# A causal attention kernel whose diagonal score blocks are laid out in quarters of 32 tokens instead of halves of 64

## The reference

```
q, k, v = heads of x @ Wq.T, x @ Wk.T, (x @ Wv.T) * sigmoid(x @ Wg.T)
q, k = rotary(rms_norm(q)) * q_gain, rotary(rms_norm(k));  k, v repeated from 4 to 16 heads
a1 = softmax(mask(q1 @ k1.T / 2)) @ v1      # mask: key <= query
a2 = softmax(mask(q2 @ k2.T / 2)) @ v2
y  = concat(a1 - lambda * a2, a1 + lambda * a2) @ Wo.T
x  = layernorm(x + y)
x  = layernorm(x + ffn(x))                  # three cycles of a small coupling network
```

## Time and profile before

| | us |
|---|---|
| median of 3 runs | 283.04 (281.01 to 283.7) |
| profiled execution, span from first to last instruction | 280.2 |
| its own time | not given |
| TensorE matmuls busy | 251.0 (90%) |
| ScalarE busy | 234.9 (84%) |
| VectorE busy | 200.2 (71%) |
| GpSimd busy | 81.4 (29%) |

### The profile page before, as it was taken

The page is one execution under the profiler, slowest core; times in us unless marked ns, Lnnn a source line. Parts: engine busy times, 40 slices in busy tenths (PEclk is TensorE's granted clock), DMA queues, the critical chain, the costliest instruction groups (busy, mean ns, idle before and its releaser), DMA issues.

```text
span 280.2 us, 8439 instructions
## 1 busy us (share of the span) xinstructions
PE 251.0 (90%) x2959; PEld 110.9 (40%) x2960; DVE 200.2 (71%) x760; ACT 234.9 (84%) x339; POOL 81.4 (29%) x241
## 2 busy tenths in 40 slices
PE   8249899999999999999999999989898999999990
PEld 3033334434344343443434444434343332223890
DVE  1687588696886967869678696773254477999993
ACT  3147899999999999999999999999975777788685
POOL 8540422415234152241522415320111000000473
PEclk9757999999999999999999999999999999999997
DMA  5201751753516526155351650615300175653045
GB/s 130 56 1 20 95 113 36 102 100 92 112 29 140 102 48 150 32 99 106 81 112 37 132 109 23 131 41 91 67 13 0 37 153 121 135 121 74 1 137 165
DMA packets 58072, 23.43 MB, mean 84 GB/s; under 512 B 42785, under 2 KB 56001, under 8 KB 58049
## 3 DMA queue, kind: packets, MB, share of 16 engines
q1 hardware_dynamic: 57760, 23.11, 39.1%
q10 hardware_dynamic: 288, 0.02, 0.1%
HBM read 4.90 MB, written 2.10 MB: 25 GB/s over the span
## 4 chain that ended last, share of the span: by engine, by line
PE 69%; issue 12%; ACT 9%; DVE 4%; DMA 2%; POOL 1%; ACTq 0%; DVEq 0%; POOLq 0%
PE O L589 11%; PE O L595 10%; PE S L713 8%; PE S L502 5%; PE S L512 4%; ACT o_sb L888 3%; PE M L628 3%; PE M L614 3%; PE S L531 3%; PE S L754 2%; DMA qk<-parts 2%; PE S L492 2%; PE S L522 2%; PE M L639 2%; PE S L723 2%
## 5 line engine op out<-in xcount | busy, mean ns | idle before, releaser
L882 ACT ACTIVATE probs_past<-S 128x1024 f32<-128x1024 f32 x64 | 64.5, 1038 | 7.1 <-PE S L492 7.1
L882 ACT ACTIVATE probs_late<-S 128x1024 f32<-128x1024 f32 x64 | 66.4, 1050 | 1.3 <-PE S L502 1.3
L589 PE MATMUL O<-probs_past,values 128*32 128x512 f32 x256 | 34.8, 612 | 7.0 <-ACT o_sb L888 5.8
L882 ACT ACTIVATE probs_early<-S 128x1024 f32<-128x1024 f32 x32 | 32.8, 1027 | 3.7 <-PE S L531 3.7
L595 PE MATMUL O<-probs_late,values 128*32 128x256 f32 x512 | 34.3, 385 | 0.2
L1130 DVE TENSOR_TENSOR roped<-rotated,rstd 128x128 f32<-128x128 f32 (+1 forms) x64 | 12.2, 247 | 26.7 <-POOL rstd L1506 26.5
L1491 POOL TENSOR_TENSOR minus_half_sum<-sum_eps,minus_half 128x40 f32<-128x40 f32 x16 | 4.5, 283 | 80.5 <-DVE estimate L1118 74.8
L1367 DVE SCALAR_TENSOR_TENSOR cY<-coup,ratio,Y 128x256 f32<-128x256 f32 x48 | 21.1, 481 | 5.8 <-ACT coup L966 5.0
L713 PE MATMUL S<-X,cn_w 128*128 128x512 f32 x48 | 25.0, 627 | 0.0
L502 PEld LDWEIGHTS S<-qk 32*64 32x64 bf16 x512 | 8.0, 101 | 34.0 <-issue 34.0
L502 PE MATMUL S<-qk 32*64 32x256 bf16 x512 | 20.2, 292 | 0.2 <-ACT probs_late L882 0.2
(11 more groups left out here) (185 smaller groups left out, 528.1 us busy)
## 6 DMA issues: line engine op xcount, KB each, us to landing
Y<-X SPq DMA_DIRECT2D x48, 128.0 KB, 2.4
xT_in<-in_xT SPq DMA_DIRECT2D x16, 128.0 KB, 2.6
x_res<-in_x SPq DMA_DIRECT2D x16, 128.0 KB, 2.1
out<-result SPq DMA_DIRECT2D x16, 128.0 KB, 1.9
qk<-parts SPq DMA_TRANSPOSE x15, 4.9
future_in<-in_future SPq DMA_DIRECT2D x1, 128.0 KB, 2.7
w_o<-in_w_o SPq DMA_DIRECT2D x2, 64.0 KB, 2.6
cn_w<-in_cn_w SPq DMA_DIRECT2D x2, 64.0 KB, 2.8
```

The costliest lines, as they stand in the source:

```text
L589: mm = pe.matmul(O[32 * g:32 * g + 32, :], values[p][:, 0, g, s, at:at + 32], probs_past[:, s, g, :], start=m == 0, stop=False)
L882: act.activation(dst, S[TILE_BUFFER[n]][:, :, :], ACT.Exp).then_inc(exp_done[n], 1)
```

## The change

The diagonal blocks are cut in quarters of 32 tokens (e = 0 to 3). The second token tile is now stored with its quarters reversed, (3, 2, 1, 0), and the first in order. Nine tiles a batch: the four LATE tiles hold, for both token tiles, the queries of the last quarter (which see all 128 keys) and one more quarter: quarter 2, which sees 96 keys. The 32 partitions of keys left over there take the first quarter of the other token tile, whose queries see only 32 keys. One MIDDLE tile holds quarter 1 (64 keys) of both token tiles for all heads. All constants for masks come in one load of 512 columns for 256; a small constant `own` (1 or 0 by partition, for three mixes) is loaded too. GpSimd's `mix_values` makes three sets of mixed values where `early_copy` made one; `early_values` and `own_half` with their memsets on VectorE go. The loop calls `middle_half` on both sides of `turn_outputs`, before weigh 2, in place of the early pair after it. ScalarE has one exponential less, and copies the heads before the last one. The code below leaves out declarations, constants and the general path.

```diff
+STORED_QUARTERS = ((0, 1, 2, 3), (3, 2, 1, 0))
-TILE_BUFFER = (0, 1, 2, 0, 1, 2, 0, 1, 0, 2)
-TILE_BEFORE = (8, 7, 9, 0, 1, 2, 3, 4, 6, 5)
+TILE_BUFFER = (0, 1, 2, 0, 1, 2, 0, 1, 2)
+TILE_BEFORE = (6, 7, 8, 0, 1, 2, 3, 4, 5)
+            sp.dma_start(own[:, :, :], A["own"]).then_inc(n_["own_loaded"], 16)
...
-            def late_part(p, n, far):
+            def late_quarter(p, n, e):
                 _, s, h = TILES[n]
                 for t in range(T):
+                    at = t * 256 + e * 128
                     for j in range(2):
                         rows = group_rows(2 * h + j)
+                        pe.matmul(S[TILE_BUFFER[n]][:, j, at:at + 128], kT[p][rows, t, s, :],
+                                  quarters(p, rows, t, s)[:, 1 - e if t else 2 + e],
+                                  start=e == 0 and t == 0, stop=False, skip_group_check=True)
+            def first_quarter(p, n):
+                _, s, h = TILES[n]
+                for t in range(T):
+                    of = 1 - t
+                    keys = slice(96, 128) if of == 1 else slice(0, 32)
+                    for j in range(2):
+                        rows = group_rows(2 * h + j)
+                        pe.matmul(S[TILE_BUFFER[n]][keys, j, t * 256:t * 256 + 128], kT[p][rows, of, s, keys],
+                                  qT[p][rows, of, :, s, keys], start=True, stop=False, skip_group_check=True)
...
+            def middle_part(p, n, h):
                 for s in range(2):
                     for t in range(T):
                         for j in range(2):
                             rows = group_rows(2 * h + j)
+                            at = (2 * h + s) * 128
+                            pe.matmul(S[TILE_BUFFER[n]][halves(t), j, at:at + 128], kT[p][rows, t, s, halves(t)],
+                                      quarters(p, rows, t, s)[:, 1 + t], start=s == 0, stop=False, skip_group_check=True)
+            def middle_mask(n, h):
+                for j in range(2):
+                    rows = halves(j)
...
+                    mm = pe.matmul(S[TILE_BUFFER[n]][:, j, h * 256:(h + 1) * 256], middle16[rows, :], quarter,
+                                   start=False, stop=True, skip_group_check=True)
...
+                    late_quarter(p, m, 0)
+                for m in (n, n + 1):
+                    first_quarter(p, m)
+                for m in (n, n + 1):
+                    late_quarter(p, m, 1)
                 for m in (n, n + 1):
                     late_mask(m)
...
+            def middle_half(b, p, n, h):
+                if h == 0:
+                    bank_free(b, n)
+                else:
+                    pe.wait_ge(n_["middle_half_done"], b + 1)
+                middle_part(p, n, h)
+                middle_mask(n, h).then_inc(scores_done[n] if h == 1 else n_["middle_half_done"], 1)
...
+                        for e in range(2):                 # weigh 2 and 3
+                            to = 3 if e == 1 else 2 * t
                             for g in range(G):
...
+                                mm = pe.matmul(O[32 * g:32 * g + 32, :].rearrange("p (r n) -> p r n", r=R)[:, :, QUARTER * to:QUARTER * to + QUARTER],
+                                               weights, probs_late[:, s, g, t * 256 + e * 128:t * 256 + e * 128 + 128],
+                                               start=False, stop=False)
...
                 late_pair(b, p, 6)
+                middle_half(b, p, 8, 0)
                 if not first:
                     turn_outputs(b - 1, project_more)
+                middle_half(b, p, 8, 1)
                 weigh(b, p, 2)
-                early_pair(b, p, 8)
...
                 exponentials(b, 7)
-                exponentials(b, 8)
                 if not first:
                     copy_heads(b - 1)
-                exponentials(b, 9)
+                exponentials(b, 8)
...
+                    last = pool.tensor_tensor(             # mix_values, for t in 0, 1
+                        mixed[p][:, :, :, :, at:at + OUTROW].rearrange("p k g s d -> p k (g s) d"),
+                        values[p][:, t, :, :, PAD:PAD + OUTROW]... .broadcast_to([128, MIXES, 2 * G, OUTROW]),
+                        own[:, t, :]... .broadcast_to([128, MIXES, 2 * G, OUTROW]), ALU.mult)
```

More of the change, by code:

```diff
@@ L511, in late_mask @@
                         rows = halves((j + h) % 2)
[L512 to L517, removed]
+                        edge = ident16[rows, rows].rearrange("p (e o n) -> p e o n", e=2, o=1).broadcast_to([EDGE, 2, R, QUARTER])
+                        mm = pe.matmul(S[TILE_BUFFER[n]][halves(1 - t), j, t * 256:(t + 1) * 256], edge16[rows, t, :], edge,
+                                       start=False, stop=True, skip_group_check=True)
+                mm.then_inc(scores_done[n], 1)
+            def middle_part(p, n, h):
                 for s in range(2):
@@ L1507, in refine, with mix_values @@
                                            ALU.mult).then_inc(n_["rstd_ready"], 1)
-            def early_copy(b, p):
+            def mix_values(b, p):
                 pool.wait_ge(n_["values_ready"], b + 1)
@@ L1526, in attend @@
                 if not last:
-                    early_copy(b + 1, 1 - p)
+                    mix_values(b + 1, 1 - p)
                 if not first:
@@ L1533, in _ @@
             refine(1)
-            early_copy(0, 0)
+            pool.wait_ge(n_["own_loaded"], 16)
+            pool.wait_ge(n_["zeros_ready"], 2)
+            mix_values(0, 0)
             refine(2)
@@ L1550 @@
 FFN_LOADS = 17
-ORDER = list(range(128)) + list(range(192, 256)) + list(range(128, 192))
+ORDER, TOKENS = ([128 * t + QUARTER * e + n for t in range(T) for e in quarters[t] for n in range(QUARTER)]
+                 for quarters in (STORED_QUARTERS, TOKEN_QUARTERS))
 def constants():
@@ L1569, in constants @@
     turn_sign = np.where((quarter == 0) | (quarter == 3), 1.0, -1.0).astype(np.float32).reshape(128, 1)
+    masks = np.zeros((128, MASKS), np.float32)
+    masks[:, 0:256] = (np.triu(np.full((SEQ, SEQ), FUTURE, np.float32), 1)[ORDER][:, ORDER]
+                       .reshape(T, 128, T, 128)[range(T), :, range(T)].transpose(1, 0, 2).reshape(128, 256))
+    triangle = np.triu(np.full((QUARTER, QUARTER), FUTURE, np.float32), 1)
+    edges = masks[:, 256:256 + 2 * EDGE].reshape(2, 2, QUARTER, T, 2, QUARTER)
+    for e, t, at in ((0, 0, 0), (0, 0, 1), (1, 0, 1), (0, 1, 0), (1, 1, 0), (0, 1, 1)):
+        edges[:, e, :, t, at, :] = triangle
+    middle = masks[:, 256 + 2 * EDGE:].reshape(2, 2, QUARTER, 4, QUARTER)
+    middle[:, 0, :, 1:3, :] = triangle[:, None, :]
+    place = np.arange(128) // QUARTER
+    own = np.zeros((128, T, MIXES), np.float32)
+    for mix, first in enumerate((3, 1, 2)):
+        own[:, 0, mix] = place < first
+        own[:, 1, mix] = place >= first
     return dict(ident=np.eye(128, dtype=np.float32), trig=np.ascontiguousarray(trig), sel_s=sel_s, turn_sign=turn_sign,
-                future=np.ascontiguousarray(np.triu(np.full((SEQ, SEQ), FUTURE, np.float32), 1)[ORDER][:, ORDER]
-                                            .reshape(T, 128, T, 128)[range(T), :, range(T)].transpose(1, 0, 2)))
+                future=masks, own=own)
 def kernel(**inputs):
@@ L1607 @@
     r = run_bass_kernel_spmd(nc, [{f"in_{k}": v for k, v in arrays.items()}], core_ids=[0])
[L1608 removed]
+    return r.results[0]["out"].reshape(BATCH, SEQ, DIM)[:, np.argsort(TOKENS)]
```

132 lines of the change are left out of this document (57 added, 75 removed).

## The result

The changed kernel is slower: 286.21 us (285.82 to 286.54, 4 runs) against 283.35, ratio 1.0118 with a 95% interval of 1.0084 to 1.0153, so 2.4 to 4.3 us. It ran again beside the last experiments: 285.91, ratio 1.0109 (1.0075 to 1.0143). The ratio is that of the mean times, 3.3 us; the medians differ by 2.9. The profiled execution took 286.54 us with a span of 284.6; the span shown of before was 280.2. The executions whose span is known took 1.8 to 2.1 us more than their span, so the profiled one of before took about 282.1 (an estimate), quick for that kernel, and the profiled one of the changed kernel is the slowest of its four. That is why the two spans differ by 4.4 us, more than the times.

The account below looks back on a forecast made before the run. TensorE's path bounds the loop: +0.34 − 0.01 + 0.06 = +0.39 us a batch, 14 times +5.5, end −0.42, together +5.0; span 280.2 to 285.2, plus 2.8 gives 288.1 us, range 280 to 293.

Parts of the forecast that it names:

- Which engine bounds: Steady loop: TensorE's chain sets the period; ScalarE follows it, with only 2.5 us of exp, exp and copy on the path.
- A shape change costs 0.14 us: TensorE groups: each takes its streaming time plus some 0.14 us where its array shape differs from the group before.
- rival 2: Late pair: shape changes within 32 rows are free, the pair takes 0.74 us, the kernel 280.5 us; chance 0.16.
- Late pair +0.17: Late scores and mask, twice a batch on TensorE's path: four groups, 1.02 us for 0.84, +0.34 a batch.
- Middle −0.01, weighs +0.06: TensorE's path: two middle halves take 0.92 us for 0.93; weigh(2) and weigh(3), in 32 records for 16, add 0.06 a batch.
- TensorE passes from group to group without waiting: Steady loop, from weigh(0) to the end of the next batch's first scores: 9.07 us of TensorE work without a wait.
- 0.3 us of slack: Before middle half 0: exp 5 ends near 109.1 us, the half comes at 109.43, so it does not wait.
- mix_values hidden: GpSimd, off the path: some 0.8 us for 0.56, covered by an idle 2.05 us before its next work.
- Start 0: Before the loop: more zeroing on GpSimd and larger loads cost 0 us, with ±0.5.
- End −0.42: End of the loop, last exp and weigh(4) on the path: the shorter weigh(4) saves 0.42 us.

Follow-up runs that it names:

- experiment 2: Kernel before with its last exponential cut to 4 of 512 columns: 282.13 us, ratio 0.9983; changed kernel with a tenth exponential: 284.76 us, ratio 1.0082.
- experiment 1: Kernel before, late pair in two groups (both score parts, then mask): 281.06 us; the same without the near part's start flag: 280.67 us, ratio 0.9936.
- experiment 3: Kernel before with every matmul of weigh 2 and 3 split in two of 128 columns: 281.60 us, ratio 0.9969.
- experiment 4: Changed kernel without first-quarter scores: 283.43 us; with late quarters together and middle masks together: 283.45; without first-quarter scores, middle halves moved later: 279.03.

## Why the prediction came out as it did

The direction, its main reason (more changes of array shape on TensorE's path) and the range held; the size was too large: +5.0 us forecast, 3.3 (2.4 to 4.3) measured, and part of the 3.3 is a fall of the clock that the forecast did not have. Step by step:

- **Which engine bounds.** Right. ScalarE's exponential was worth nothing in both directions (experiment 2).
- **A shape change costs 0.14 us.** Right, and shown with the same instructions in another order (experiment 1): 0.15. That 32x128 to 32x32 and back costs it as well, which no row had shown, is in the chain of the changed kernel: pair 0.98, forecast 1.02, with 0.74 if rival 2 held. By the Trainium skill ("TensorEngine Tiling (Array Packing)", Key Properties) a change of tiling mode drains the TensorE; the trace agrees in that each change costs time, 0.15 us.
- **Late pair +0.17.** Measured +0.14: 128 columns on 32x32 add 0.18, not 0.20.
- **Middle −0.01, weighs +0.06.** Measured −0.03 and +0.02. The loads are hidden at 128 columns too (experiment 3): 32 records in 1.01 us. The rule of the Trainium skill ("TensorE: Matmul & The Clock Gate", Part 3, The mechanism) that loads overlap running matmuls only when the row group differs does not hold for these loads, which all use the 128 rows.
- **"TensorE passes from group to group without waiting."** This step failed. Weigh(1) did wait, 0.04 us for exponential 3 (107.16 in experiment 1), and its group then took 1.06 in place of the 0.99 that it takes without a wait: 0.11 us of the path belonged to ScalarE. The first late pair's +0.14 was laid over it, so the period rose by 0.19 and not by 0.27, the sum of the measured parts (2 x 0.14 − 0.03 + 0.02); 0.27 − 0.11 is 0.16, and the rest is rounding and a few hundredths in the other links. Experiment 1 shows the same from the other side: what the first pair saves is not seen. Sized so, the forecast for the loop would have been 14 x 0.19 = 2.7 in place of 5.5.
- **"0.3 us of slack" before middle half 0.** 0.06 by the trace, since TensorE came 0.15 sooner after weigh(0) than I had summed (4.39 for 4.54), and exponential 5 let it go at 4.33. It cost nothing in the changed kernel, but it is why no shortening of the late pairs could bring the period down there (experiment 4).
- **mix_values hidden.** Right in effect: two operations of 415 ns; VectorE's `roped` beside them went from 247 to 302 ns, in front of a wait that took it up. That the longer operation slows it was seen, not isolated.
- **Start 0.** Batch 1 began 0.15 later: the transposing DMA was issued 0.17 earlier but took 6.38 us for 6.06.
- **End −0.42.** Wrong: +0.22. Weigh(4) did shrink, but I had not asked what was late next: VectorE's chain to x1 of batch 14.
- **The clock.** Not in the forecast. Halving weigh(4) took TensorE's work out of a stretch where, without a projection, there is little else: idle 1.28 us for 1.06. That this brought the fall is likely, not shown.

That 5.0 came near the 4.4 between the two spans is luck: 2.8 too much in the loop, against 0.6 at the end, 1.4 for the clock and 0.15 at the start too little.

## What to carry to other kernels

Count the changes of array shape, not the columns: with groups of eight to sixteen small matmuls a change costs more than halving the columns saves, and putting groups of one shape side by side is a gain if their start flags allow it, as far as no wait behind them takes it back. When two engines are both nearly full, here 97% and 95% of the period, look for the places where the shorter path touches the longer (here exponential 3 and exponential 5): time saved ahead of such a point is not seen, nor is time added there as long as it only fills the wait, and behind it both count in full. Ask of every shortened piece what is late next, also at the last pass of a loop.

## What the runs showed of the hardware that was not expected

- The granted clock can fall inside the loop: to 0.50 for 3 us after two microseconds with TensorE busy 0.49 and 0.23 of each, and in another execution a batch later. Other kernels with the same 1.28 us of idle time had no fall in their profiles.
- A weigh of 32 records takes 1.01 us where 16 take 1.00: with weights on 128 rows and 32 columns, a record of 128 columns streams for some 107 ns (853 ns in eight waves; four such records take 0.44 us in L614), and the next loads, 110 ns each in the profile, are hidden behind it. Loads are under way in 0.81 us of the 1.01.
- VectorE's f32 multiply with a broadcast operand was 22% slower (247 to 302 ns, mean of 64) in the kernel where GpSimd's operation beside it had grown from 32 to 120 elements. No run isolates this.
